# A vision layer on one core: scores from split features, a new order of all engines, a router by max and index instructions

## The reference

```python
s = s * float(d) ** (-0.25);  s = einsum('bhld,fd->bhlf', s, omega)
diag = sum(s, axis=-1, keepdims=True) / 2.0
m = max(s, axis=-1) if query else max(s, axis=(1, 3))     # keepdims
feature = F ** (-0.5) * (exp(s - diag - m) + 1e-6)
rhs = cumsum(kf[..., None, :] * vl[..., :, None], axis=0)  # over the 256 tokens
a = einsum('lbhdf,lbhf->lbhd', rhs, qf);  denom = einsum('lbhf,lbhf->lbh', qf, cumsum(kf, axis=0))
out = (a / (denom + EPS)) @ w_out[0] + b_out
```

## Time and profile before

| | |
|---|---|
| median of 3 runs | 936.08 us (936.07 to 937.3) |
| profiled execution | 934.5 us, its span 932.8 us |
| granted TensorE clock, mean | 0.865 |
| busy share of the span | PE 82%, PEld 71%, DVE 59%, ACT 43%, POOL 48% |
| token stage | 0 to about 95 us |
| attention | about 95 to 542 us |
| experts | from about 542 us |

### The profile page before, as it was taken

The page is one execution under the profiler, slowest core; times in us unless marked ns, Lnnn a source line. Parts: engine busy times, 40 slices in busy tenths (PEclk is TensorE's granted clock), DMA queues, the critical chain, the costliest instruction groups (busy, mean ns, idle before and its releaser), DMA issues. The chain is left out here.

```text
span 932.8 us, 17076 instructions
## 1 busy us (share of the span) xinstructions
PE 764.9 (82%) x4751; PEld 657.9 (71%) x4752; DVE 547.5 (59%) x1729; ACT 403.9 (43%) x821; POOL 447.1 (48%) x441
## 2 busy tenths in 40 slices
PE   3970689999999999999999306999997899999950
PEld 2560467786767777776767306999997899999950
DVE  2130344676766777676666624888789665565530
ACT  1130343433444444343433004777765566656630
POOL 7733222244444333334442333777775666666542
PEclk9795589888888888898888558999999999999995
DMA  7122211111111121111100002333332234434337
GB/s 169 21 76 98 84 39 58 59 57 33 46 47 49 58 58 58 58 58 58 49 21 21 20 9 58 55 62 63 56 63 40 46 66 77 75 77 76 61 44 138
DMA packets 62448, 55.07 MB, mean 59 GB/s; under 512 B 24616, under 2 KB 55791, under 8 KB 62399
## 3 DMA queue, kind: packets, MB, share of 16 engines
q0 software_dynamic: 19840, 23.53, 14.8%
q1 hardware_dynamic: 38079, 27.77, 10.6%
q10 hardware_dynamic: 4480, 3.21, 1.0%
HBM read 32.52 MB, written 25.10 MB: 62 GB/s over the span
## 5 line engine op out<-in xcount | busy, mean ns | idle before, releaser
L1079 POOL DMA_INDIRECT result<-e_y,e_tag x78 | 137.6, 1764 | 97.1 <-DVE e_y L1408 85.2
L478 POOL DMA_INDIRECT tbl_dram<-a_entry,a_slot x64 | 63.4, 991 | 200.5 <-DVE a_token L926 163.0
L1137 PE MATMUL e_yp<-x_w2s,e_hh 128*128 x468 | 139.4, 365 | 2.0 <-DVE e_y L1408 2.0
L1401 DVE TENSOR_TENSOR e_hl<-e_hid,e_hh 128x512 fp32r<-128x512 f32 x117 | 80.2, 689 | 88.7 <-ACT e_hh L1203 88.5
L1195 ACT ACTIVATE e_hid<-e_hidden,e_b 128x256 f32<-128x256 f32 x234 | 101.2, 475 | 55.0 <-PE e_hidden L1124 39.9
L1138 PE MATMUL e_yp<-x_w2s,e_hl 128*128 x468 | 117.5, 251 | 0.0
L517 PE MATMUL a_s<-a_qb_t,a_kf_t 128*128 128x512 f32 x192 | 110.4, 705 | 0.0
L529 PEld LDWEIGHTS a_ab<-a_values,a_masked 128*128 128x128 f32 x768 | 95.4, 192 | 6.8 <-issue 4.5
L1203 ACT CAST e_hh<-e_hid 128x512 fp32r<-128x512 f32 x117 | 72.4, 621 | 61.8 <-PE e_yp L1138 61.8
L1067 POOL DMA_INDIRECT e_x<-x_dram,e_tag x78 | 81.7, 1048 | 36.3 <-issue 22.9
L529 PE MATMUL a_ab<-a_values,a_masked 128*128 (+1 forms) x768 | 95.0, 256 | 0.6 <-DVE a_masked L768 0.6
(11 more groups left out here) (254 smaller groups left out, 1619.6 us busy)
## 6 DMA issues: line engine op xcount, KB each, us to landing
a_raw_c<-in_ew SPq DMA_DIRECT2D x16, 288.0 KB, 3.1
h_dram<-t_hs SPq DMA_DIRECT2D x4, 768.0 KB, 4.2
a_hb<-h_dram SPq DMA_DIRECT2D x16, 192.0 KB, 2.7
a_raw_a<-in_ew SPq DMA_DIRECT2D x16, 192.0 KB, 2.4
a_raw_b<-in_ew SPq DMA_DIRECT2D x32, 96.0 KB, 2.6
result<-a_hb SPq DMA_DIRECT2D x16, 192.0 KB, 2.0
x_dram<-a_att SPq DMA_DIRECT2D x16, 192.0 KB, 2.0
spec_dram<-e_space ACTq DMA_DIRECT2D x16, 192.0 KB, 2.0
```

The source lines that it names most:

```text
L1079: pool.indirect_dma_start(out=out, in_=y[:, j], in_offset=None, out_offset=bass.IndirectOffsetOnAxis(ap=tag[:, i % 8, j, 0:1].bitcast(U32) ...
L1137: pe.matmul(Y[:, j, 0:2 * D], hh[:, f, c], w(f, 2 * D), start=f == 0, stop=False, skip_group_check=True)
L1401: g.tensor_tensor(hl[:, f:f + 2].rearrange("p f t -> p (f t)"), hid[:, f:f + 2].rearrange("p f t -> p (f t)"), hh[:, f:f + 2].rearrange("p ...
```

## The change

**Token stage.** The identity is made in a tile `made` and copied by POOL to an f32r tile `ident_r` ahead of the gathers. The three parts of W1 are made here and no longer in the attention loop: SP loads one expert after another into a ring of 4 in the space of `hs`, ACT rounds (2 copies of 768 elements for each expert), DVE subtracts (2). Expert 0 stands ahead of group t1, experts 1 to 7 ahead of p2 and p1. The first copies of h wait for the last of them.

**Attention.** The features are no longer padded. ACT adds the epsilon after its exp, then rounds the features to f32r in tiles `split` of three parts for each head, and POOL subtracts to get the low part: queries have (high, low, high), keys (high, high, low). Two heads with three parts of 16 make 96 rows. PE turns these with 24 plain f32r matmuls against the identity, ACT copies them out (queries twice, each time with one head's rows scaled to zero by `own_head`), and a score is two f32r matmuls of 96 x 128 weights by 256 columns. The state has two groups of 6 heads, and its mask by DVE closes the iteration. The values' copy goes from DVE to ACT. The choice is made by `max` and `max_index` from the logits in PSUM and one exp of the difference of the two largest; the count is kept in bf16 and the prefix has four small matmuls. Every engine has a new order: PE puts a score between other work, and POOL scatters first in an iteration, then computes rstd2, the low parts and rstd1. SP loads h ahead of W2. Six PSUM banks are regrouped.

**Experts.** Only the count's sum (two bf16 matmuls) and the name of the identity differ.

```diff
 def tokens_block
+            for e in range(NE):
+                if e >= RING:
+                    sp.wait_ge(w1_low, 2 * (e - RING + 1))
+                sp.dma_start(raw_a[:, e % RING], of_expert(slice(0, P), e)).then_inc(raw_in[e % RING], 16)
+                for r in (0, EMB):
+                    sp.dma_start(raw_b[r:r + EMB, e % RING], of_expert(slice(P, D), e)).then_inc(raw_in[e % RING], 16)
...
+            pool.wait_ge(const_ready, 2)
+            nc.gpsimd.tensor_copy(ident_r[:], made[:]).then_inc(const_ready, 1)
...
+        weights_before = {("t1", 0): (0,), ("t1", 1): (0,), ("p2", 0): range(1, NE), ("p1", 0): range(1, NE)}
...
+                    if k < 2:
+                        eng.wait_ge(w1_low, 2 * NE)
...
+            def low_parts(e):
+                dve.wait_ge(w1_high, 2 * e + 1)
+                dve.tensor_tensor(w1l[:, e], raw_a[:, e % RING], w1h[:, e].bitcast(F32), ALU.subtract).then_inc(w1_low, 1)
+                dve.wait_ge(w1_high, 2 * e + 2)
+                dve.tensor_tensor(w1s[EMB:P, e], raw_b[EMB:P, e % RING], w1s[EMB:P, e].bitcast(F32), ALU.subtract
+                                  ).then_inc(w1_low, 1)
...
+            def high_parts(e):
+                act.wait_ge(raw_in[e % RING], 48 * (e // RING + 1))
+                act.copy(w1h[:, e], raw_a[:, e % RING]).then_inc(w1_high, 1)
+                act.copy(w1s[:, e], raw_b[:, e % RING]).then_inc(w1_high, 1)
...
 attention_block, POOL
+                if tail:
+                    rstd("rstd2_ready", i - 2, mv2, rstd2, "tail", 5 * (i - 2) + 4)
+                if one:
+                    low_part(i, 0)
+                    if not (fixed(i) and i == B - 1):
+                        rstd("rstd1_ready", i + 1, mv, rstd1, "norm_step", 5 * (i + 1) + 4)
+                    low_part(i, 1)
...
 PE
-                def scores(g):
-                        pe.matmul(S[j][:].rearrange("p h t -> p (h t)"), kf_t[:, g, j * P:(j + 1) * P],
-                                  qb_t[:, g, j].rearrange("p h t -> p (h t)"), start=True, stop=True
+                def score(n):
+                    g, j = n // 2, n % 2
+                    if n < 2:
+                        pe.wait_ge(s["kT_out"], TJ * b + j + 1)
+                        pe.wait_ge(s["qT_out"], TJ * b + j + 1)
+                    if not (fixed(i) and i == 1) or n >= 2:
+                        pe.wait_ge(s["s_out"], 6 * b + n - 1)
+                    for p in range(2):
+                        last = pe.matmul(S[j][:, 2 * p:2 * p + 2].rearrange("p h t -> p (h t)"),
+                                         kf_t[:, 2 * g + p, j * P:(j + 1) * P],
+                                         qb_t[:, 2 * g + p, j].rearrange("p h t -> p (h t)"), start=True, stop=True)
+                    last.then_inc(s["s_done"], 1)
...
+                def turn_keys(j):
+                    for n in range(NP):
+                        last = pe.matmul(FB[0:CF, n * P:(n + 1) * P],
+                                         split[j][:, H + 2 * n:H + 2 * n + 2].rearrange("p h c f -> p (h c f)"),
+                                         ident_r[:], start=True, stop=True)
+                    last.then_inc(s["kT_done"], 1)
...
 ACT
+                    act.activation(feat[j][:], feat[j][:], ACT.Exp).then_inc(s["exp_done"], 1)
+                    act.wait_ge(s["exp_done"], 4 * i + 2 * j + 1)
+                    act.activation(feat[j][:], feat[j][:], ACT.Identity, bias=eps_col[:, 0:1]).then_inc(s["exp_done"], 1)
...
+                    for n, at in ((0, slice(0, 3, 2)), (1, slice(0, 2))):
+                        own = slice(n * H, (n + 1) * H)
+                        act.copy(split[j][:, own, at], feat[j][:, own].unsqueeze(2).broadcast_to([P, H, 2, NF])
+                                 ).then_inc(s["hi_ready"], 1)
...
+                    for r in range(2):
+                        last = act.activation(qb_t[:, :, j, r], FA[0:CF, 0:NP * P].rearrange("p (n t) -> p n t", n=NP),
+                                              ACT.Copy, scale=own_head[:, r:r + 1])
+                    last.then_inc(s["qT_out"], 1)
...
 DVE
+                for j in range(TJ):
+                    v.max(out=best[:, j], in_=lg[:, j, 0:NE]).then_inc(s["found"], 1)
+                wait_apart(dve, s["found"], 4 * b + 2)
+                for j in range(TJ):
+                    v.max_index(out=where[:, j], in_max=best[:, j], in_values=lg[:, j, 0:NE]).then_inc(s["found"], 1)
```

More of the change, by code:

```diff
@@ L222, in copy_out @@
                 ps = bank[n % 8]
+                for e in weights_before.get((what, k), ()):
+                    weights(e)
                 if what == "t1" and k == par and par == 0:
@@ new lines, in turn_queries @@
+                def turn_queries(j):
+                    for n in range(NP):
+                        last = pe.matmul(FA[0:CF, n * P:(n + 1) * P],
+                                         split[j][:, 2 * n:2 * n + 2].rearrange("p h c f -> p (h c f)"),
+                                         ident_r[:], start=True, stop=True)
+                    last.then_inc(s["qT_done"], 1)
+                if two:
+                    score(0)
+                if choice:
+                    pe.wait_ge(s["chosen_ready"], i - 2)
+                    if not fixed(i) or i >= 4:
+                        pe.wait_ge(s["counted"], i - 3)
+                    pe.wait_ge(s["state_out"], known(i))
+                    pe.wait_ge(s["logit_out"], i - 2)
+                    all_of = M[:, 0:TJ * NE].rearrange("p (j e) -> p j e", j=TJ)
+                    pe.matmul(all_of, before[:], chosen[:], start=True, stop=False)
+                    for j in range(TJ):
+                        pe.matmul(all_of, ones[:], count[:, j].unsqueeze(1).broadcast_to([P, TJ, NE]), start=False, stop=False)
+                    pe.matmul(M[:, NE:2 * NE], ones[:], chosen[:, 0], start=False, stop=True).then_inc(s["prefix_done"], 1)
@@ L596, in emit @@
+                    last.then_inc(s["v_done"], 1)
                 if two:
[L597 removed]
+                    score(3)
                 if one:
[L599 to L600 removed]
                     qk(1)
[L602 to L603 removed]
                 if two:
[L605 to L606 removed]
+                    average(1)
@@ new lines, in emit @@
+                if tail:
+                    pe.wait_ge(s["xn2_ready"], i - 1)
+                    pe.wait_ge(s["v_out"], known(i + 1))
+                    if not one:
+                        pe.wait_ge(s["kT_out"], TJ * B)
+                    turn(R[3], xn2).then_inc(s["xn2T_done"], 1)
+                if two:
+                    score(4)
+                    average(2)
+                if tail:
+                    pe.wait_ge(s["xn2T_out"], i - 1)
+                    pe.wait_ge(s["state_out"], known(i))
+                    if choice:
+                        pe.wait_ge(s["slots_ready"], i - 2)
+                    for j in range(TJ):
+                        for c in range(2):
+                            last = pe.matmul(M[:, 2 * CV + j * (NE + 1):2 * CV + (j + 1) * (NE + 1)],
+                                             xn2_t[0:KH + c, c, j * P:(j + 1) * P], w_gate[0:KH + c, c],
+                                             start=c == 0, stop=c == 1)
+                    last.then_inc(s["logit_done"], 1)
@@ L693, in emit @@
                 if one:
+                    features(1)
+                    keys_out(0)
+                    queries_out(0)
+                    keys_out(1)
+                if tail:
+                    act.wait_ge(s["gap_ready"], i - 1)
+                    act.activation(prob[:], gap[:], ACT.Exp).then_inc(s["prob_ready"], 1)
+                if one:
+                    act.wait_ge(s["qf_done"], i + 1)
+                    act.wait_ge(s["qT_done"], TJ * (i + 1))
                     if two:
-                        act.wait_ge(s["av_done"], 6 * i)
@@ L738, in apply1 @@
             def apply1(b):
[L739 removed]
+                if not (fixed(b) and b == 0):
                     dve.wait_ge(s["xnT_done"], b)
```

633 lines of the change are left out of this document (282 added, 351 removed).

## The result

The changed kernel is slower: the median of four executions is 957.9 us (948.7 to 968.5) against 936.1. So the change costs 1.5% to 2.3%. The forecast was 918.6, faster. The time lies inside the stated range of 882 to 975, on the wrong side of 936. The profiled execution took 952.5 us, 18.0 more than the 934.5 of before.

What follows compares the result with a forecast made beforehand. PE's pass list was taken as the bound: 17.49 work + 1.44 waits + 5.75 clock = 24.68 us an image. Thirteen images (-11.1), -0.6, -6, +0.5, -0.3 from 934.5 gave 917.0, plus 1.6: 918.6 us, range 882 to 975.

Steps and rivals of the forecast that it cites:

- The work on PE: Attention loop: PE's passes sum to 17.49 us an image at the upper clock level, 3.25 less than before.
- The waits: Attention loop: PE's waits stay at 1.44 us an image, with 0.6 and 4 as bounds.
- The cover that I worried about: Attention loop: xn2 is ready some 1.5 us before PE wants it, although POOL scatters before computing rstd2.
- The clock: Attention loop: slow clock costs PE 5.75 us an image, the middle between 3.4 and 8.1; called the largest unknown.
- as before: Attention loop, a rival: clock stays low only as long as before, 3.4 us lost an image, 887.8 us; chance 0.18.
- all narrow work behind 4.6 us is slow: Attention loop: clock falls 4.6 us after the wide passes and stays low until the rise, 8.1 us lost an image.
- My own sign of being wrong: Attention loop: forecast wrong if granted clock is above 0.83 or below 0.72, or PE idles over 3 us an image.
- late* rival: Attention loop: 256-column scores do not raise the clock, projection and first qk run slow, image 28.63, 973.6 us; chance 0.23.
- another limit binds: Attention loop: rstd2 comes 3 us too late or narrow f32r turns cost 0.215, image about 27.8, 959 us; chance 0.10.
- The token stage: Before the loop: making W1's parts on ACT and DVE adds 0.5 us (0 to 4), partly hidden by ACT's 3.67 idle.
- The end: From the last image's first qk to the last scatter: 6 us shorter, bounds -14 and +3.
- The short choice: Last choice at the loop's end: DVE's small steps of 4.6 us become about 1.5, saving 3; sign: under 2 us.

Runs made afterwards that it cites:

- the run with eight wide passes: The changed kernel plus two f32r matmuls of 512 columns ahead of each of scores 0, 1, 4 and 5: 911.8 us against 935.7 before.
- the fastest run: The changed kernel's own order, W1 split moved, passes added at gate logits and averages 2 to 5: 896.8 us, 0.960 times the kernel before.
- the second order with added passes: The changed kernel reordered (qk, projection, values early; averages singly behind), W1 split moved, wide and f32 passes added at scores and averages: median 965.0 us.
- the first order: The changed kernel with PE's pieces reordered, DVE and POOL following, nothing added or left out: 926.1 us, 0.989 times the kernel before.

## Why the prediction was wrong

**The work on PE was right within 0.4 us.** 17.49 us an image was the sum. In the image at 289 us the lower level covers 20.5 of 27.36 us (1.9 before 290.9, 1.24 of the two from 297, 17.4 behind), so 10.2 are lost and 17.1 are the work. Its terms were less exact: score 2, a pair of passes, took 0.55 (291.02 to 291.57) for my 0.24, and the other scores of this image at the upper level 0.37 and 0.32, while values took 1.17 for 1.30 and an average 0.81 to 0.83 for 0.86. Six turned features took 0.54 at the upper level (273.29 to 273.83 in the run with eight wide passes), 0.09 each for my 0.086.

**The waits were wrong, for the better.** I kept 1.44 us; PE idles 0.15 us an image. The cover that I worried about (scatters ahead of rstd2) was never used up. A PE at half speed comes late to everything, which may be why; no run tested it.

**The clock is the step that failed.** I took 5.75 us, the middle between "as before" (3.4) and "all narrow work behind 4.6 us is slow" (8.1). The 3.4 is what the clocks of the earlier trace rows give for 6.84 us at 0.50: 0.15 + 3.00 + 0.27. Measured: 10.2 in the image above and 9.3 on the average (at 0.65 the lower level holds 0.70 of 26.5 us, and half of that is lost). That is above my upper bound for two reasons. Projection and part of qk ran slow too, 2.56 and 2.0 us for 1.39 and 1.38, which is 1.8 us. And the clock fell at about 297.8, 3.3 us behind the last wide pass (294.48) and not 4.6, which is 1.3 more; with the 7 us of narrow work that I had, 10.1. It rose at 290.9, 1.9 us into the 408-column passes of qk, while scores 0 and 1 in their new form and the projection of 192 columns ahead of it had run at the lower level. My own sign of being wrong, a clock below 0.72 in the loop, came true with 0.65.

This is the mechanism of the *late* rival, worked out at 9.7, to which I gave 0.23. Its image of 28.63 was 2.15 too long: 1.3 by the waits that vanished, 0.4 by the work and 0.4 by the clock, 28 us in 13 images. Outside the loop it was 8 too short, 6 of them in the token stage, so that it came out 20 too high for the profiled execution and 16 for the median. The rival *another limit binds* named 959, 1 us from the median, and that is luck: its conditions were turns of 0.215 or a long wait for the scatters, and the turns cost 0.09 and PE waits 0.15 us an image. The evidence for a late return had been in the rows: before, the clock came back 1.2 us into four passes of 512 columns, and the change takes just these away. I noted it and put a middle value on it, though no row lay near the middle.

The middle does exist, for other images of the same execution:

```profile
343.73 0.89 PE L578 MATMUL a_fa<-a_wqkv,a_xn_t 96*128 96x408 f32 x1
...
368.02 0.89 PE L578 MATMUL a_fa<-a_wqkv,a_xn_t 96*128 96x408 f32 x1
...
389.89 0.51 PE L578 MATMUL a_fa<-a_wqkv,a_xn_t 96*128 96x408 f32 x1
...
414.10 0.89 PE L578 MATMUL a_fa<-a_wqkv,a_xn_t 96*128 96x408 f32 x1
```

24.3, 21.9 and 24.2 us stand between intervals of 27.4. What made these three images differ, with the same instructions as the others, is not known. The shortest takes 20% less than the usual one, and the four executions of the changed kernel lie 20 us apart, those of the kernel before beside them 2. That the number of such images makes that difference was not tested.

**Idle gaps and the clock.** A PE that is fed without a gap does not keep the upper level here: the window 299 to 317 has it idle for 0.03 us of 18 and the clock at 0.50, as the six busy microseconds of the earlier trace rows had. In the two runs with waits (1.33 and 0.69 us) a fall followed each wait, but they do not show that the wait was the cause: the fastest run has waits of 0.25 and 0.6 us with a fall behind them in one image and none in the next. It was right to take the slow stretch from the row; it was wrong to stop at "unknown".

**The token stage** was the second miss, +6.2 for +0.2 (+0.5 less the 0.3 of the constants). The term put at nearly nothing is the chain by which W1 gets in: expert 0's parts wait for its load ahead of t1, and from expert 4 on ACT waits again for each load (1.42 to 1.66 us), which starts only when DVE is done with that place of the ring. ACT's row of the last expert:

```profile
46.90 0.83 ACT L298 CAST x_w1h<-t_hs 128x768 fp32r<-128x768 f32 x1 [1.55 <-DMA t_hs<-in_ew]
```

I had priced the casts (1.1 us, measured 0.83) and called the rest hidden by one idle stretch of 3.67 us. But the groups behind them came so late that this stretch is gone. Moving the split won back part of it, as shown above; that the rest is this chain too is argued from the timeline.

**The end** gained 3.9 of the 6. The short choice came out as planned: from its first instruction to the count it took some 1.8 us (550.5 to 552.3) for 4.7. The clock was 0.56 from 475 to 560 us, where before it was 0.73 from 475 to 541.

## What to carry to other kernels

A change that makes PE's passes fewer and narrower can lower PE's clock and lose more by it than it saves (here the clock of the loop went from 0.87 to 0.65 and an image from 25.53 to 26.48 us): cost it twice, at both levels, and ask which passes lift the clock today and whether the change removes them. Where a value lies between two states of a switch, forecast the states and not their middle. If nothing wide is left to do, a few useless wide passes at the place where the trace shows the fall can pay for themselves: here 2.7 us of added passes, 1.8 of them wide, made an image 4.2 us shorter. Compare a trace with several others of the same code before you read 2 or 3 us out of it: the same token stage ended 3.3 us apart in six traces.

## What the runs showed of the hardware

- Adding PE work made the kernel faster by 42 to 45 us (four f32r passes of 512 columns an image), and four f32 matmuls of 17 columns in the same places did not (+2 to +9 us). One of the first adds 0.23 us at the upper level, one of the second 0.14.
- A PE that is busy without a gap ran at a granted clock of 0.50 for 18 us (299 to 317 in the changed kernel). There are falls with a wait of 0.7 to 1.3 us ahead of them (0.69 in the second order with added passes, 1.33 in the first order) and falls with none (297.8 in the changed kernel, with PE busy for all of 291 to 299, and 274 in the run with eight wide passes, with PE busy for all of 261 to 274).
- An average of four f32 matmuls of 128 weight columns by 17 costs 0.81 to 0.86 us at the upper level, in bf16 0.11 to 0.12 (210.35 to 210.46, 213.32 to 213.44): more than the factor of two of the passes, x8 and x4 in the traces.
- Seven gathers that POOL issues took 1.55 to 1.68 us and not 0.95 in the changed kernel, six beside DVE's subtractions of 768 elements and one (26.35) beside its copy of 1536 elements. Not every gather beside a subtraction did: those at 32.11 and 33.37 took 0.95. Without the subtractions one of 1.54 is left, beside the copy. Rows of POOL and DVE in the changed kernel:

```profile
36.49 1.67 POOL L164 DMA_INDIRECT t_g<-in_x,t_idx  x1 [0.30 <-issue]
...
40.43 0.95 POOL L164 DMA_INDIRECT t_g<-in_x,t_idx  x1 [0.30 <-issue]
```

```profile
36.37 0.96 DVE L287 TENSOR_TENSOR x_w1l<-t_hs,x_w1h 128x768 fp32r<-128x768 f32 x1
37.36 0.95 DVE L289 TENSOR_TENSOR x_w1s<-t_hs,x_w1s 64x768 fp32r<-64x768 f32 x1
...
41.49 0.96 DVE L287 TENSOR_TENSOR x_w1l<-t_hs,x_w1h 128x768 fp32r<-128x768 f32 x1 [1.20 <-ACT x_w1h L298]
```
